# A two-layer kernel: ranking set apart from the router, two products issued in parts, and heads normalised one slot later

## The chip, the cores and the metric

The kernel runs on one core of a Trainium2 chip, as one launch. The metric is the device time in microseconds from the first to the last instruction, as a median over runs. Five engines work side by side, each through its own list of instructions: TensorE (PE, with its weight loads as PEld), VectorE (DVE), ScalarE (ACT), GpSimd (POOL) and SyncE (SP), which here only issues transfers. They wait for each other on semaphores alone.

## What is computed

Two layers over x of 8 batches, 512 rows and 128 columns, all in 32-bit floats. A layer normalises its rows, computes a sequence part s and a gate part g, and gives x + s * silu(g). In the first layer s is a state-space scan with 16 states and g a mixture of 8 experts, 2 for each row. In the second layer s is a causal attention of one head; g is a block of its own, cut to what matters here:

```
x = x + attention(rmsnorm(x, w_ln1))          # 16 heads, keys shared, causal softmax, product with Wo
residual = x
xn = rmsnorm(x, w_ln2)
probs = softmax(xn @ Wgate + expert_bias)     # 8 experts
topk_p, topk_i = top_k(probs, 2)
topk_p = topk_p / sum(topk_p)
comb = sum(one_hot(topk_i) * topk_p)
routed = einsum(comb, experts(xn))            # silu(xn @ Wg) * (xn @ Wu), then @ Wd
g = residual + shared_expert(xn) + routed
out = x_of_the_layer + s * silu(g)
```

The ratio of two softmax values does not depend on the softmax's denominator, and the order of the values doesn't either.

## The kernel before

`two_layers` has three stages with barriers between them: `route` and `experts0` (the first layer's routing and experts, and the scan of the first three batches), and `layer1`, in which the scan of batches 3 to 7 and the whole second layer run together. The change is in `layer1` and in `top_two`, which it calls.

`layer1` is written out as a list of slots, 24 for each batch (`SLOTS`), and each engine walks through the same slots in the same order, from `SLOT0` to `SLOT1`. A slot from 0 to 191 does one sixth of a quad of heads: four heads of one batch are a quad, and a batch has four quads. In each slot PE computes two score tiles into bank 1 (`scores`), two tiles from which the maxima of a quad 8 slots ahead are taken into bank 0 (`maxima`), and adds the masks to both. Then ScalarE does the exponential (L1519), and DVE the reduce of the maxima (L1709). There is one bank for each, so `scores` of the next slot waits for the exponential and `maxima` for the reduce. Every second slot PE multiplies the probabilities with the values (`weigh`, L1264).

Everything else of a batch is attached to a slot by the table `WHEN`, relative to the batch's slot 0: `due(slot, what)` gives the batch for which `what` is due in this slot. With 24 slots to a batch, an entry of 34 falls into the next batch's slot 10. In this text "loop batch n" is the slots 24n to 24n+23, and "place p" is a slot whose number modulo 24 is p. In a slot, each engine issues what is due in the order of its own code, behind the slot's scores and maxima. An engine works its list strictly in order, so that a wait holds up all that stands behind it.

What the change touches, with its place before:

- Head quads. ScalarE copies a finished quad to `o` (`take_quad`), SP copies its denominators to `dens` (`denominators`, 7 slots after the quad's first, `DENS`), DVE inverts them (L1766, 8 slots, `INVERT`), SP writes them to memory and reads them back, spread over 128 partitions (`spread_reciprocals`, 8 slots, `SPREAD`), and DVE multiplies (L1769, 10 slots, `TAKE`: places 4, 10, 16 and 22). `o` holds `HEADS_KEPT` quads.
- `attention` (29, place 5): PE waits for all four normalised quads of a batch and multiplies them with `wvo` in 32 matmuls (L1381) into bank 5; DVE adds the rows (L1809) and gives `x2`.
- `squares`, `roots2`, `scale2`, `turn2` (30, 30, 31, 32): second norm and its transpose (L1298).
- `router` (34, place 10): logits by 8 matmuls (L1408); on DVE `top_two`: bias, maximum, subtraction (L1838 to L957), ScalarE's exponential (L1590), sum, reciprocal, product (L959 to L961), the pairwise comparison and rank (L964 to L969), the gates and their normalisation (L973 to L976).
- `gates_a` to `ups_c` (38 to 41): expert products through banks 5, 6 and 7, with silus on ScalarE (L1547), which needs another table than the exponential.
- `down` (46, place 22): 40 matmuls (L1324) into bank 5, then DVE's addition to `x2` (L1882).
- `final`, `result` (47, 48) and `average1` (0): the last steps of a batch on ScalarE and DVE; DVE's result is L1885 to L1887, that of the average L1893. `store` and `fetch_x` on SP wait for the result.
- The scan on DVE: four steps in every four slots (L291, L298, L308, L315), as long as batches 3 to 7 last, up to slot 148. `SCAN_PIECES` says at which slot and through which bank its projections go; `scan_due` looks it up.

`claim(n, taker, count)` makes PE wait until the last user of bank n has read it. `late` shifts the end of batch 6 by three slots, past the last scores.

## Time and profile before

| | |
|---|---|
| median of 3 runs | 1313.63 us |
| lowest and highest run | 1307.95 and 1328.43 us |
| span of the profiled execution | 1322.4 us |
| PE busy | 1105.6 us (84%) |
| DVE busy | 976.9 us (74%) |
| ACT busy | 623.9 us (47%) |
| POOL busy | 297.1 us (22%) |

The profile is of one execution, somewhat longer than the median one. Busy time is an instruction's own time on its engine; "idle before" an instruction, and the releaser named with it, say for whom the engine stood still. Matmul ends are modelled, so small overlaps mean nothing. The second layer's slots begin at about 406 us.

### The profile page before, as it was taken

What the parts mean: (1) busy time and instruction counts of PE and PEld (TensorE: products, weight loads), DVE (VectorE), ACT (ScalarE), POOL (GpSimd) and SP (SyncE); (2) the same over time, 40 slices, a digit from 0 to 9 for tenths busy, and PEclk for the clock granted to TensorE, in tenths of its full rate; (3) what the DMA queues carried; (4) which work ended last, traced back from release to release, by engine and by line L of the source; (5) the groups of instructions that cost most, each with busy time, mean ns of one, the idle gap of its engine ahead of it and who ended that gap; (6) DMA issues with size and microseconds to landing.
All of it is one profiled execution on the core that took longest, in us unless ns stands there. A gap on an engine that the chain in (4) does not pass through costs nothing.

```text
span 1322.4 us, 19242 instructions
## 1 busy us (share of the span) xinstructions
PE 1105.6 (84%) x6765; PEld 689.4 (52%) x6765; DVE 976.9 (74%) x1514; ACT 623.9 (47%) x1111; POOL 297.1 (22%) x370
## 2 busy tenths in 40 slices
PE   7679999998767977888789888988988888898886
PEld 6567787787334434435444543543455354455353
DVE  6748878886488776986897698799889867654433
ACT  2647667663325424455346454553544543443421
POOL 2075555550313103202020320141032201000000
PEclk9779999999888878988899898998999989899898
DMA  7568777773363433253235325424533421310010
GB/s 201 162 217 250 234 221 232 231 223 100 98 127 98 113 81 95 78 118 102 64 96 120 108 77 102 119 78 111 114 112 87 102 48 34 57 42 19 17 50 8
DMA packets 91117, 150.24 MB, mean 114 GB/s; under 512 B 21032, under 2 KB 50032, under 8 KB 90960
## 3 DMA queue, kind: packets, MB, share of 16 engines
q1 hardware_dynamic: 67888, 72.33, 21.6%
q0 software_dynamic: 22976, 76.43, 19.3%
q8 instruction: 56, 0.92, 0.3%
q10 hardware_dynamic: 160, 0.26, 0.2%
q14 instruction: 37, 0.30, 0.1%
HBM read 124.33 MB, written 11.54 MB: 103 GB/s over the span
## 4 chain that ended last, share of the span: by engine, by line
PE 26%; DVE 22%; issue 9%; DMA 7%; ACT 7%; POOL 2%; another core or an unknown queue 2%; SPq 0%; DVEq 0%; POOLq 0%; ACTq 0%
PE bank L1235 5%; DVE neg_max L1709 4%; DMA rec_wide<-head_recips 3%; DVE sc_state L298 2%; ACT probs L1519 2%; PE bank L1264 2%; PE bank L1319 2%; PE bank L1381 2%; PE bank L1315 2%; PE bank L1283 2%; PE bank L1324 2%; PE bank L1241 2%; PE bank L1306 1%; ACT L1519 1%
## 5 line engine op out<-in xcount | busy, mean ns | idle before, releaser
L1519 ACT ACTIVATE probs<-bank 128x1024 f32<-128x1024 f32 (+1 forms) x192 | 169.1, 881 | 337.9 <-PE bank L1241 238.4
L1709 DVE TENSOR_REDUCE neg_max<-bank 128x2 f32<-128x1024 f32 (+3 forms) x256 | 204.2, 819 | 110.7 <-PE bank L1241 80.7
L1235 PE MATMUL bank<-q_all,kk 49*128 49x512 f32 (+3 forms) x1024 | 204.1, 498 | 49.2 <-ACT probs L1519 39.4
L212 POOL DMA_DIRECT2D sc_bc_wide<-scan_bc x128 | 73.1, 572 | 492.6 <-DVE sc_ub L291 254.7
L1235 PEld LDWEIGHTS bank<-q_all,kk 49*128 49x128 f32 x1024 | 88.1, 197 | 156.7 <-issue 66.5
L1283 PE MATMUL bank<-kr,q_all 48*128 48x512 f32 (+3 forms) x512 | 114.0, 481 | 51.3 <-DVE neg_max L1709 49.7
L779 PE MATMUL bank<-xcol,wst 128*128 128x256 f32 x624 | 149.7, 384 | 0.6 <-issue 0.6
L298 DVE TENSOR_TENSOR_SCAN sc_state<-sc_a,sc_ub 128x1024 f32<-128x1024 f32 x64 | 146.0, 2282 | 0.0
L900 POOL DMA_INDIRECT xrow<-sorted_in,token_of x78 | 103.1, 1322 | 120.5 <-PE bank L766 63.3
L779 PEld LDWEIGHTS bank<-xcol,wst 128*128 128x128 f32 x624 | 114.1, 193 | 13.6 <-issue 0.9
L1264 PE MATMUL bank<-probs,vaug 128*32 128x512 f32 (+3 forms) x1024 | 99.8, 487 | 0.0
L1283 PEld LDWEIGHTS bank<-kr,q_all 48*128 48x128 f32 x512 | 49.5, 203 | 90.4 <-DVE neg_max L1709 69.7
L925 DVE SCALAR_TENSOR_TENSOR hid<-bank,wst,gel 128x256 f32<-128x256 f32 x156 | 67.4, 474 | 37.4 <-issue 24.1
L291 DVE TENSOR_TENSOR sc_ub<-sc_u,sc_bc_wide 128x1024 f32<-128x1024 f32 x64 | 78.0, 1218 | 15.6 <-DMA sc_bc_wide<-scan_bc 13.7
L250 ACT ACTIVATE sc_a<-sc_dt,neg_a 128x511 f32<-128x511 f32 x128 | 84.2, 711 | 5.7 <-PEq L682 4.3
L795 PE MATMUL bank<-w,hid 128*128 x624 | 84.7, 279 | 0.5 <-DVE hid L925 0.5
L1663 POOL DMA_INDIRECT expert_out<-sorted_out,slot x64 | 72.0, 1125 | 55.2 <-POOLq L138 35.2
L795 PEld LDWEIGHTS bank<-w,hid 128*128 128x128 f32 x624 | 77.3, 191 | 11.4 <-issue 7.6
L854 ACT ACTIVATE gel<-bank,wst 128x256 f32<-128x256 f32 x156 | 64.5, 476 | 23.1 <-PE bank L779 21.1
L315 DVE TENSOR_TENSOR sc_y<-sc_y,sc_ub 128x1024 f32<-128x1024 f32 x56 | 68.1, 1216 | 0.0
L308 DVE TENSOR_TENSOR sc_ub<-sc_state,sc_bc_wide 128x1024 f32<-128x1024 f32 x56 | 68.0, 1215 | 0.0
L1678 POOL TENSOR_SCALAR mean_sq<-ssq 128x4 f32<-128x4 f32 x8 | 7.2, 899 | 175.6 <-ACT work_b L1576 175.2
(300 smaller groups left out, 1809.6 us busy)
## 6 DMA issues: line engine op xcount, KB each, us to landing
sc_bc_wide<-scan_bc POOLq DMA_DIRECT2D x128, 512.0 KB
wst<-in_wexp SPq DMA_DIRECT2D x39, 512.0 KB
q_all<-q_kind SPq DMA_DIRECT2D x94, 128.0 KB, 4.4
rec_wide<-head_recips SPq DMA_DIRECT2D x31, 256.0 KB
p_t<-gates_turned SPq DMA_DIRECT2D x14, 512.0 KB
sorted_out<-xrow SPq DMA_DIRECT2D x7, 640.0 KB
rows_all<-in_x SPq DMA_DIRECT2D x8, 256.0 KB, 4.4
sorted_in<-rows_all SPq DMA_DIRECT2D x8, 256.0 KB, 5.6
```

What stands on the lines that cost most here:

```text
L212: eng.dma_start(self.v["bc_wide"][:, n % 2, what, :, :], self.bc_d[b, first:first + PER, :].partition_broadcast(P)).then_inc(self.rows_in[ ...
L250: last = self.nc.scalar.activation(self.v["a"][:, n % 2, j, 1:L], self.v["dt"][:, 1:L], ACT.Exp, scale=self.neg_a[:, state:state + 1])
L291: self.nc.vector.tensor_tensor(v["ub"][:], v["u"][:].unsqueeze(1).to_broadcast([P, PER, L]), v["bc_wide"][:, n % 2, 0, :, :], ALU.mult).th ...
L298: self.nc.vector.tensor_tensor_scan(merged(v["state"][:]), merged(v["a"][:, n % 2, :, :]), merged(v["ub"][:]), 0.0, ALU.mult, ALU.add).the ...
L779: last = mm(bk(inner(m)[half])[:, i * ROWS:(i + 1) * ROWS], wst[:, w % WB, half * FF + f * P:half * FF + (f + 1) * P], xcol[:, w % 3, :], ...
L795: last = mm(bk(5)[:, r * P:(r + 1) * P], hid[:, m % 4, i, r * P:(r + 1) * P], w2[:, bass.ds(e * FF + f * P, P)], start=False, stop=(f == F ...
L900: nc.gpsimd.indirect_dma_start(out=xrow[:, m, :], out_offset=None, in_=xs[0:B * L], in_offset=bass.IndirectOffsetOnAxis(ap=t["token_of"][: ...
L1235: mm(bank[1][:, par, at:at + n], kk[rows, b % 2, kt * P:(kt + 1) * P], q_all[rows, quad // 2 % 3, pair, kt * P:L].bitcast(F32), start=(at ...
L1264: last = mm(bk(4)[row:row + 32, kt * P:L], vaug[:, b % 2, kt, :], probs[:, (6 * quad + 2 * kg + pr) % RING, par, at:at + L - kt * P], star ...
L1283: mm(bank[0][:, par, at:at + n], q_all[rows, quad // 2 % 3, pair, i * P:(i + 1) * P], kr[rows, b % 2, 0:n], start=(at == 0), stop=False)
L1519: af(probs[:, slot % RING, :, 0:width], bank[1][:, :, 0:width], ACT.Exp, scale=0.125).then_inc(s["p_ready"], 1)
L1709: last = v.tensor_reduce(neg_max[:, quad % 2, pr:4:2, i], bank[0][:, :, at:at + (i + 1) * P], AX, ALU.max, negate=True)
```

## The change

Seven edits to the order of the second layer, in one diff:

- `top_two` is divided. The shift of the logits stays with the router, which moves from 34 to 36. The rest is due at 38 (`rank`). Sum, reciprocal and product of the softmax are left out; the final normalisation of the two gates stays.
- `attention` becomes `heads_a` (27: three quads, 24 matmuls) and `heads_b` (30: the fourth quad, 8 matmuls), both into bank 5, of which only the first matmul has the start flag. The second norm's steps move one slot later.
- `INVERT`, `SPREAD` and `TAKE` become 9, 9 and 11; `HEADS_KEPT` 5, `ROWS_KEPT` 3.
- `dens` and `recs` are 128x16 in place of 32x64, and so is their copy in memory.
- `down` becomes `down_a` (46, 20 matmuls) and `down_b` (47, 20 matmuls); `final` and `result` move to 48 and 49.
- `average1` moves from 0 to 1.
- Banks: the turned rows go through 7 in place of 5, the up products through 5, 6, 7 in place of 7, 5, 6, and two scan projections leave bank 5. `turned_rows` shrinks, and the last batch's turned gates use a part of `kk`.

```diff
-        rec_d = nc.dram_tensor("head_recips", (B * 4, 32, 64), F32, kind="Internal").ap()
+        rec_d = nc.dram_tensor("head_recips", (B * 4, P, 16), F32, kind="Internal").ap()
...
-def top_two(v, dve, link, t, s, normalise, turn=0):
+def shift_logits(v, link, t, s):
+
+    prob, small = t["prob"], t["small"]
+    link(v.tensor_reduce(small[:, :, 0:1], prob[:], AX, ALU.max))
+    v.tensor_tensor(prob[:], prob[:], small[:, :, 0:1].to_broadcast([P, J, E]), ALU.subtract).then_inc(s["shifted"], 1)
+
+
+def top_two(v, dve, link, t, s, turn):
...
-    link(v.tensor_reduce(small[:, :, 0:1], prob[:], AX, ALU.max))
-    v.tensor_tensor(prob[:], prob[:], over(0), ALU.subtract).then_inc(s["shifted"], 1)
     dve.wait_ge(s["exp_ready"], turn + 1)
-    link(v.tensor_reduce(small[:, :, 1:2], prob[:], AX, ALU.add))
-    link(v.reciprocal(small[:, :, 2:3], small[:, :, 1:2]))
-    link(v.tensor_tensor(prob[:], prob[:], over(2), ALU.mult))
...
-    qk1=-6, scores1=-5, turn1=-3, average1=0,
-    attention=29, squares=30, roots2=30, scale2=31, turn2=32, router=34, gates_a=38, gates_b=39, ups_a=39, ups_b=40, ups_c=41,
-    turn_gates=41, gate_hidden=44, down=46, final=47, result=48)
+    qk1=-6, scores1=-5, turn1=-3, average1=1,
+    heads_a=27, heads_b=30, squares=31, roots2=31, scale2=32, turn2=33, router=36, rank=38, gates_a=38, gates_b=39, ups_a=39, ups_b=40, ups_c=41,
+    turn_gates=41, gate_hidden=44, down_a=46, down_b=47, final=48, result=49)
...
-HEADS_KEPT = 4
-ROWS_KEPT = 2
-
-DENS, INVERT, SPREAD, TAKE = 7, 8, 8, 10
+HEADS_KEPT = 5
+ROWS_KEPT = 3
+
+DENS, INVERT, SPREAD, TAKE = 7, 9, 9, 11
...
-        dens, recs, rec_wide = sb("dens", [32, 64]), sb("recs", [32, 64]), sb("rec_wide", [P, L])
+        dens, recs, rec_wide = sb("dens", [P, 16]), sb("recs", [P, 16]), sb("rec_wide", [P, L])
...
+                def heads_part(to, b, g, j):
+                    return mm(to[:, j * P:(j + 1) * P], o[:, (4 * b + g) % HEADS_KEPT, j * P:(j + 1) * P], wvo[:, g, :],
+                              start=(g == 0 and j == 0), stop=(g == 3 and j == J - 1))
+
...
-                    if (b := due(slot, "attention")) is not None:
+                    if (b := due(slot, "heads_a")) is not None:
                         to = claim(5, s["x2_ready"], b + 1)
+                        pe.wait_ge(s["yn_ready"], 4 * b + 3)
+                        for j in range(J):
+                            for g in range(3):
+                                heads_part(to, b, g, j)
+                    if (b := due(slot, "heads_b")) is not None:
                         pe.wait_ge(s["yn_ready"], 4 * (b + 1))
                         for j in range(J):
-                            for g in range(4):
-                                last = mm(to[:, j * P:(j + 1) * P], o[:, (4 * b + g) % HEADS_KEPT, j * P:(j + 1) * P], wvo[:, g, :], start=(g == 0), stop=(g == 3))
+                            last = heads_part(bk(5), b, 3, j)
                         last.then_inc(s["att_psum"], 1)
...
-                        up_part(b, 1, 7)
-                        up_part(b, 2, 5)
-                        up_part(b, 3, 6)
+                        up_part(b, 1, 5)
+                        up_part(b, 2, 6)
+                        up_part(b, 3, 7)
...
-                        for j in range(J):
-                            last = down_part(b, j, to)
+                        for j in range(J // 2):
+                            down_part(b, j, to)
+                    if (b := due(slot, "down_b")) is not None and b != B - 2:
+                        for j in range(J // 2, J):
+                            last = down_part(b, j, bk(5))
                         last.then_inc(s["moe_psum"], 1)
...
+                    if (b := due(slot, "rank")) is not None:
+                        if b >= 1:
+                            dve.wait_ge(s["gates_psum"], b)
+                        dve.wait_ge(s["rope_ready"], 4 * min(b + 3, B))
+                        top_two(v, dve, link, dict(prob=prob, small=small, rank=rank, gates=gates, cmp_a=cmp_a, cmp_b=cmp_b, c=c), s, b)
```

## Rows read from the trace of the kernel before

**Rows 1.** The page's part 4, the chain that ended last, shares by engine.

```profile
PE 26%; DVE 22%; issue 9%; DMA 7%; ACT 7%; POOL 2%; another core or an unknown queue 2%; SPq 0%; DVEq 0%; POOLq 0%; ACTq 0%
```

**Rows 2.** Busy time by stretches: stretch, length, then each engine, granted clock, DMA.

```profile
core 0: us, PE busy (x) PEld busy (x) DVE busy (x) ACT busy (x) POOL busy (x), PEclk, DMA share, GB/s
800.00:900.00 100.00, 86.91 (x561) 47.25 (x561) 83.51 (x124) 53.15 (x88) 22.00 (x26) 0.95 0.41 104
...
1100.00:1200.00 100.00, 88.60 (x609) 49.46 (x607) 60.96 (x106) 43.33 (x74) 4.14 (x8) 0.97 0.20 41
```

**Rows 3.** One line over the run: durations (min/median/max), first and last start.

```profile
L1519 ACT ACTIVATE probs<-bank x192: 577/1023/1036, 406.0 to 1273.1; 128x1024 f32<-128x1024 f32 x128, 128x512 f32<-128x512 f32 x64
```

**Rows 4.** Timeline, slots 82 to 84 (start, length, operation, [idle before <-releaser]).

```profile
795.78 1.13 PE L1408 MATMUL bank<-c_router,work_b 128*128 128x128 f32 x8 [0.45 <-ACT turned_rows L1531]
...
800.81 0.18 DVE L1838 TENSOR_TENSOR prob<-bank,c_bias 128x32 f32<-128x32 f32 x1
...
801.47 0.23 ACT L1590 ACTIVATE prob<-prob 128x32 f32<-128x32 f32 x1 [5.84 <-DVE prob L957]
...
802.40 0.42 DVE L964 TENSOR_TENSOR turned<-prob 128x256 f32<-128x256 f32 x1
...
805.23 0.19 DVE L976 TENSOR_TENSOR gates<-gates,small 128x32 f32<-128x32 f32 x1
805.34 1.28 DVE L1709 TENSOR_REDUCE neg_max<-bank 128x2 f32<-128x768 f32 x2
...
806.68 0.58 PE L1283 MATMUL bank<-kr,q_all 48*128 48x256 f32 x2 [2.30 <-DVE neg_max L1709]
```

**Rows 5.** Timeline of DVE and ScalarE, slots 86 and 87 (places 14 and 15).

```profile
822.57 0.54 DVE L1766 RECIPROCAL recs<-dens 32x64 f32<-32x64 f32 x1 [1.50 <-DMA dens<-o]
824.04 0.69 DVE L1709 TENSOR_REDUCE neg_max<-bank 128x2 f32<-128x512 f32 x1 [0.93 <-PE bank L1241]
...
823.03 1.28 ACT L1519 ACT_TABLE_LOAD   x1
```

**Rows 6.** Timeline of PE in loop batch 7, slots 179 and 180.

```profile
1228.76 1.13 PE L1235 MATMUL bank<-q_all,kk 49*128 49x512 f32 x4 [0.81 <-ACT probs L1519]
...
1233.11 0.58 PE L1283 MATMUL bank<-kr,q_all 48*128 48x256 f32 x2 [3.21 <-DVE neg_max L1709]
```

**Rows 7.** Timeline of PE, slot 88 (place 16).

```profile
829.85 2.84 PE L1319 MATMUL bank<-work_b,c_wu 128*128 128x512 f32 x6 [0.82 <-ACT turned_rows L1531]
```

**Rows 8.** Timeline of PE and DVE, slots 94 to 98 (places 22 to 2).

```profile
853.88 1.23 DVE L1709 TENSOR_REDUCE neg_max<-bank 128x2 f32<-128x1024 f32 x1 [0.38 <-PE bank L1241]
...
855.23 4.70 PE L1324 MATMUL bank<-c_wd,hm 128*128 128x128 f32 x40
...
859.97 0.69 DVE L1882 TENSOR_TENSOR x<-x,bank 128x512 f32<-128x512 f32 x1 [2.90 <-issue]
...
861.91 1.29 DVE L1709 TENSOR_REDUCE neg_max<-bank 128x2 f32<-128x768 f32 x2 [1.26 <-PE bank L1243]
...
873.24 0.96 DVE L1709 TENSOR_REDUCE neg_max<-bank 128x2 f32<-128x768 f32 x1 [0.72 <-PE bank L1243]
```

**Rows 9.** Timeline at place 5, in loop batch 3 and in loop batch 7.

```profile
770.88 3.81 PE L1381 MATMUL bank<-wvo,o 128*128 128x128 f32 x32 [1.29 <-DVE o L1769]
...
1205.02 0.69 DVE L1769 TENSOR_TENSOR o<-o,rec_wide 128x512 f32<-128x512 f32 x1 [2.15 <-DMA rec_wide<-head_recips]
...
1205.85 5.42 PE L1381 MATMUL bank<-wvo,o 128*128 128x128 f32 x32 [1.73 <-DVE o L1769]
```

**Rows 10.** Groups by line and shape on DVE: count, busy us, mean ns, idle before.

```profile
L1766 DVE RECIPROCAL recs<-dens 32x64 f32<-32x64 f32 x31 | 16.6, 535 | 19.1 <-DMA dens<-o 19.1
...
L1758 DVE RECIPROCAL prob<-bank 128x16 f32<-128x16 f32 x1 | 0.3, 258 | 0.7 <-PE bank L1335 0.7
```

**Rows 11.** Timeline of PE, slot 80 (place 8): transposes of the second norm's rows.

```profile
786.59 0.66 PE L1298 MATMUL bank<-c_ident,work_a 128*128 128x128 f32 x4
```

**Rows 12.** Transfers by line: count, size each, median us from issue to landing.

```profile
head_recips<-recs SPq DMA_DIRECT2D x31, 8.0 KB, 1.4
...
c_a_log<-in_a_log SPq DMA_DIRECT2D x1, 8.0 KB, 2.3
```

36 lines of the change are left out of this document (15 added, 21 removed).

## The prediction

> **What bounds the kernel now.** I read, in this order: the chain that ended last, the busy time by stretches, the list of one line over the whole run, the timeline of one loop batch (batch 3, slots 72 to 95), and the same places in the last loop batch. The chain [rows 1] has no owner: PE 26%, DVE 22%, and both hand over to each other. The stretches [rows 2] say why: between 800 and 900 us DVE is busy 83.5 of 100 us and PE 86.9 of 100. After 1100 us, where the scan has ended, DVE falls to 61 of 100 and PE stays at 88.6. The 192 slots of the second layer run from 406.0 to 1273.1 us [rows 3]: 867 us, 4.5 us a slot, 108 us for a loop batch of 24 slots. Only these slots and the tail behind them are touched; the first 406 us are not.
>
> A slot has one score bank and one bank for the maxima. PE can't write the maxima of slot s+1 before DVE has reduced those of slot s, and DVE reaches that reduce only behind everything that was queued on it in slot s-1. So a slot lasts as long as the longer of PE's and DVE's work in it, with a lag of about one slot allowed. What is to be looked for is where one of the two stands still because the other has a lump. I name a place by the slot's number modulo 24.
>
> **The change, part by part.**
>
> *Ranking (places 10 and 11 before; router at 12, ranking at 14 after).* Before, the block goes on DVE from 800.81 to 805.42 us: 4.61 us, of which 0.66 us (until ScalarE takes over at 801.47) is the shift of the logits, and 3.02 us (802.40 to 805.42) the ranking proper [rows 4]. Between them lie 0.93 us: the wait for ScalarE's exponential, and sum, reciprocal and product, which are dropped. The reduce of slot 83 stands behind all that, and PE, which has been through its own work of the slot, waits 2.30 us for it [rows 4]. ScalarE waits 5.84 us for the shifted logits before it may do the exponential of slot 83, so the scores of the next slot are late as well. After, 4.61 - 0.66 = 3.95 us leave these places. The shift comes back at place 12, with the router's eight matmuls, 1.13 us [rows 4], ahead of the queries that DVE turns there; DVE will wait about that long for the queries. 3.95 - 1.13 = 2.82 us; but PE had only 2.30 us of idleness there, and its latents and values become the longer side, so I take 2.3 us.
> The 3.02 us of ranking go to place 14. There ScalarE sets the slot: two table loads around three silus, until the exponential that follows 823.03 + 1.28 us. DVE stands idle 1.50 us, does a reciprocal of 0.54 us that moves to place 15, and stands idle 0.93 us more [rows 5]: 2.97 us of room for 3.02 us. Cost about 0.1 us. So 2.2 us in each of loop batches 1 to 6 (the first ranking falls in loop batch 1): 13.2 us. Bounds for one batch: 0.93 us (what is dropped, if the moved part pushes as much elsewhere) and 3.95 us.
> In loop batch 7 no scan, queries or latents share the places. There PE waits 0.81 us for ScalarE and 3.21 us for DVE [rows 6]: 4.0 us go.
>
> *Banks of the up products (place 16).* The first up product wants bank 7, which the turned maxima have just filled: PE waits 0.82 us for ScalarE's copy [rows 7]. With bank 5 it doesn't wait. The slot's exponential is PE's to release, and the normalisation that stood on DVE in this slot moves to place 17, in front of a slot whose length PE sets. I take the whole 0.82 us, in seven loop batches: 5.7 us. Lower bound 0.
>
> *Down product in halves (places 22, 23), result and average at place 1.* The 40 matmuls take 4.70 us, DVE waits 2.90 us for their end and then 1.26 us for the next maxima [rows 8]. Half of the product, 2.35 us, goes to place 23, which is short on PE. But a normalisation and the addition (0.69 us each, as the row of L1882) go there too, behind a scan step, and three operations of the result go to place 1, which was short and is then full on DVE. From the reduce at 853.88 to that at 873.24 us the four slots take 19.4 us. I take about half of the 2.35 us, 1.2 us, in loop batches 1 to 6: 7.2 us. Bounds 0 and 4.16 us a batch.
>
> *Heads in 3/4 and 1/4, normalised a slot later.* Before, PE waits 1.29 us for the normalised heads and does 32 matmuls in 3.81 us [rows 9]. In this stretch, though, DVE works without a gap (the average input of the next batch stands behind the normalisation), so PE's stall is beside the chain: 0 in loop batches 1 to 6, where 24 matmuls, 3/4 of 3.81 = 2.9 us, now lie in place 3 under a scan step. In loop batch 7 DVE has nothing of that kind and PE is the chain: its wait of 1.73 us goes [rows 9]. Bounds: a loss of 0.5 us a batch (place 3 becomes PE's) and a gain of 1.29 us.
>
> *Small parts.* The reciprocal has 128x16 for 32x64: 258 ns against 535 ns, both sizes being in the trace [rows 10]. 31 times 0.277 us is 8.6 us of DVE, but only those that land at places 3 and 9 lie where DVE is the chain; 15 or 16 of them, 4.3 us. Against it, the turn of the second norm's rows (0.66 us [rows 11]) now stands ahead of the queries of place 9, seven times: 4.6 us at most. I put the two together at 0. The bank swaps of the turned rows and of two scan pieces only keep clear of bank 5, now held from place 3 to 6, and a third row buffer and a fifth head buffer keep the later use from blocking the norm: 0. In the tail, where one batch runs alone, the three dropped operations are on the chain: 0.7 us.
>
> *The queues.* SyncE's order changes at places 1, 3, 9, 15 and 21: the fetch of the next rows and, behind it, the copy of the denominators now wait for the result at place 1. The reciprocal wants them two slots later, some 10 us, so I cost it at nothing; if that cover were gone, DVE's reduce of place 3 would be late next.
> The denominators' copies become 128 pieces of 64 bytes for 32 of 256. The write of the reciprocals lands in 1.4 us now, and a load of the new form, 128x16, took 2.3 us [rows 12]. I take 0.9 us more, hidden: two slots lie between inversion and use. The Trainium skill (DMA: Bandwidth & Descriptors, Specifications) says that below 512 bytes a transfer is off line rate and pays a read-modify-write; the trace has both sizes below that. By the Trainium skill the new form could only be slower; by the row the sum stays as it is unless the round trip outgrows its two slots.
>
> **The sum.** 13.2 + 4.0 + 5.7 + 7.2 + 1.7 + 0 + 0.7 = 32.5 us, from the profiled execution's span of 1322.4 us: 1289.9 us. That execution lies 0.7% above the median of the runs, 1313.6 us, whose lowest is 1308.0. So I expect 1313.6 - 32.5 = 1281 us. About 2% (26 us, below 1287.4 us) is what a measurement of this kernel can tell from no change.
>
> **The rivals.**
> 1. *DVE keeps the bound and only removed work counts.* For: DVE is busy over 83% and its lumps move, they don't vanish. Against: its waits at places 14, 22 and 23 are real idleness next to lumps. Worth 7 x 0.93 + 5.7 + 4.3 = 16.5 us: 1297 us.
> 2. *The holes close fully.* PE's stalls and DVE's both vanish, with 3.95 us a batch for the ranking, 2.35 us for the down product and the 2.4 us of loop batch 7's heads and the tail: 7 x 3.95 + 5.7 + 6 x 2.35 + 2.4 = 50 us, 1264 us. Against: PE is as busy as DVE, and can't give more than it waits.
> 3. *Slower: the denominators' round trip.* If each of the 31 trips (copy, inversion, write, broadcast) becomes 4 us longer while its slack is 2 us, DVE, in whose order the normalisation stands, waits 2 us each time: 62 - 32 = 30 us more, 1344 us. It makes the kernel slower from 1.1 us of uncovered wait a trip on. For: DVE waits for this broadcast already, 2.15 us in loop batch 7 [rows 9]. Against: 8 KB took 2.3 us in the new form, 0.9 us more and not 4 [rows 12]. The Trainium skill's rule named above speaks for it too.
> 4. *Nothing moves:* what leaves places 10 and 22 is given back at 3, 12 and 1, in slots that PE then sets. PE at 87% busy speaks for it. About 1310 us.
>
> **How the numbers follow.** Forecast 0.50 (its own range 1270 to 1291), rival 1 0.29, rival 2 0.08, rival 3 0.05, rival 4 0.08. The likeliest gives 1281 us. With 2 in 10 left out (rival 3, rival 4 and the far end of rival 2) the range is 1262 to 1305 us: below it everything would have to close, above it less than 9 us would be left. Faster by over 2% (under 1287.4): most of the forecast's 0.50, rival 2 and a little of rival 1, 0.54. Within 2%: 0.40. Slower by over 2%: rival 3 beyond its point and unforeseen waits, 0.06.
>
> **What the profile will show.** Right: no wait of PE at the reduce of place 11, ScalarE's exponential of the logits without its 5.84 us; the ranking ending within 0.2 us of the reduce of place 15; no wait for the turned maxima at place 16; DVE's wait at place 22 about halved; the heads in two groups, the second without a wait; reciprocals at 258 ns; DVE busy 86 to 88% between 800 and 900 us. Wrong: waits on the denominators or the broadcast over 20 us each in sum; place 12 longer by more than the 1.8 us of router and shift; place 3 with DVE idle over 1 us; place 1 with PE waiting for the average's bank; or a lower granted clock than the 0.95 and 0.97 of [rows 2].

## The result, and the profile after it

The changed kernel takes 1303.4 us (median of 20 runs, 1295.4 to 1310.4) against 1316.2 us before (20 runs in the same sessions). The ratio is 0.990, 95% interval 0.988 to 0.993: 12.6 us less, where the forecast was 32.5. The profiled execution has a span of 1302.6 us against 1322.4.

First the totals of the page of the changed kernel: span, busy time, and the chain that ended last, by engine.

```profile
span 1302.6 us, 19217 instructions
PE 1100.2 (84%) x6765; PEld 690.9 (53%) x6765; DVE 962.8 (74%) x1490; ACT 623.5 (48%) x1111; POOL 303.6 (23%) x370
PE 32%; DVE 15%; DMA 10%; issue 7%; ACT 6%; POOL 3%; SPq 1%; DVEq 0%; POOLq 0%; ACTq 0%
```

Against [rows 1] VectorE fell from 22% to 15% of the chain, as wanted, but TensorE rose from 26% to 32% and DMA from 7% to 10%. Which transfer it is stands in the waits of the changed kernel (us in total, times, longest), and in the page's group of its score matmuls (busy us, mean ns, idle just before, and what ended it):

```profile
PE bank L1234 <- DMA q_all<-turned_rows: 47.4, 21, 6.3
```

```profile
L1234 PE MATMUL bank<-q_all,kk 49*128 49x512 f32 (+3 forms) x1024 | 205.3, 500 | 70.8 <-DMA q_all<-turned_rows 47.4
```

TensorE waits 47.4 us in 21 places, 6.3 us at most, for the copy of the turned maxima's rows into the queries' buffer (two transfers of 4 KB, each with the rows of two heads). In the kernel before that wait was 6.0 us in three places:

```profile
PE bank L1235 <- DMA q_all<-turned_rows: 6.0, 3, 2.5
```

The rows are turned at places 4, 10, 16 and 22 and needed by the scores two slots later. The change moves neither this copy nor its user; what stood around them moved. 25.2 of the 47.4 us lie ahead of place 6, in loop batches 1 to 7; the rest lies ahead of places 0 (5.8 us), 12 (6.5 us) and 18 (9.9 us).

The longest case is ahead of place 6 of loop batch 3. SyncE's queue and TensorE, changed kernel:

```profile
758.93 0.34 SPq L1144 DMA_DIRECT2D head_recips<-recs  x1
762.17 0.57 SPq L1149 DMA_DIRECT2D rec_wide<-head_recips  x1
762.79 1.36 SPq L1133 DMA_DIRECT2D q_all<-turned_rows  x2
```

```profile
760.60 0.38 PE L1242 MATMUL bank<-mask,ident 128*128 128x256 bf16 x2
767.29 2.08 PE L1234 MATMUL bank<-q_all,kk 49*128 49x512 f32 x4 [6.31 <-DMA q_all<-turned_rows]
768.38 1.21 PE L1282 MATMUL bank<-kr,q_all 48*128 48x256 f32 x2
771.02 1.16 PE L1328 MATMUL bank<-wvo,o 128*128 128x128 f32 x8
```

ScalarE has turned the rows by 759.92, but SyncE stands in `spread_reciprocals`: it wrote the reciprocals at 758.93 and may issue their broadcast only when they have landed, at 762.17 (3.2 us, the longest of the 31; the median is 1.4 us). The rows come behind that. In the kernel before the broadcast was issued a slot earlier, and at place 5 TensorE had the 3.81 us of the heads' product [rows 9] while the rows travelled. Now 3/4 of that product lie in place 3 and 1/4 in place 6 (771.02), and place 5 is empty.

This stall has a second price. Busy time by stretches, changed kernel, columns as in [rows 2] (the granted clock is the third number from the end):

```profile
759.00:761.00 2.00, 1.98 (x25) 1.04 (x17) 2.00 (x2) 1.33 (x2) 0.00 (x0) 1.00 0.07 12
761.00:767.30 6.30, 0.01 (x2) 0.01 (x2) 6.04 (x16) 3.94 (x6) 2.48 (x4) 0.75 0.12 43
767.30:770.00 2.70, 2.70 (x10) 1.19 (x10) 1.33 (x5) 0.05 (x1) 2.20 (x4) 0.50 0.01 3
770.00:772.00 2.00, 2.00 (x18) 1.18 (x17) 1.82 (x2) 1.57 (x2) 0.00 (x0) 0.77 0.73 233
```

Before the stall TensorE has 2.4 GHz. While it stands idle the grant falls, and behind the stall it works at 0.50, which is 1.2 GHz, on the scores and maxima of place 6: four score matmuls take 2.08 us there and 1.13 us in the next slot. VectorE then waits 1.53 us for the maxima. Where [rows 2] had a clock of 0.95 and 0.97, the same stretches now have 0.93 and 0.94:

```profile
800.00:900.00 100.00, 88.67 (x568) 49.02 (x568) 81.89 (x123) 54.09 (x89) 22.90 (x27) 0.93 0.37 100
1100.00:1200.00 100.00, 92.74 (x627) 52.62 (x625) 54.55 (x88) 43.25 (x74) 1.20 (x2) 0.94 0.20 42
```

Over the whole execution the mean grant is 0.909, for 0.922 before. That isn't the doing of this wait alone: e4_invert8 below has a third of it and 0.906.

What the change was for, by contrast, is there (TensorE, ScalarE and VectorE, loop batch 3; changed kernel):

```profile
802.08 0.23 ACT L1600 ACTIVATE prob<-prob 128x32 f32<-128x32 f32 x1 [1.01 <-DVE prob L951]
814.72 0.20 DVE L975 TENSOR_TENSOR gates<-gates,small 128x32 f32<-128x32 f32 x1
816.08 0.69 DVE L1719 TENSOR_REDUCE neg_max<-bank 128x2 f32<-128x512 f32 x1 [1.16 <-PE bank L1240]
820.92 2.74 PE L1318 MATMUL bank<-work_b,c_wu 128*128 128x512 f32 x6
849.23 2.47 PE L1323 MATMUL bank<-c_wd,hm 128*128 128x128 f32 x20
852.84 2.40 PE L1323 MATMUL bank<-c_wd,hm 128*128 128x128 f32 x20
```

ScalarE waits 1.01 us for the shifted logits, not 5.84 [rows 4]; the up product has no wait, for 0.82 [rows 7]; the down product comes in halves, for 4.70 us in one piece [rows 8].

### The profile page after: what moved, and what is told of

The parts are those of the page before. It is cut to its first block, busy times and chain, and to the rows that moved or that the text cites. A ratio compares the mean times of both kernels' runs of the same rounds, so it can differ in the third digit from the quotient of the medians.

```text
span 1302.6 us, 19217 instructions
## 1 busy us (share of the span) xinstructions
PE 1100.2 (84%) x6765; PEld 690.9 (53%) x6765; DVE 962.8 (74%) x1490; ACT 623.5 (48%) x1111; POOL 303.6 (23%) x370
## 3 DMA queue, kind: packets, MB, share of 16 engines
q1 hardware_dynamic: 73840, 72.33, 22.5%
## 4 chain that ended last, share of the span: by engine, by line
PE 32%; DVE 15%; DMA 10%; issue 7%; ACT 6%; POOL 3%; SPq 1%; DVEq 0%; POOLq 0%; ACTq 0%
PE bank L1234 7%; DMA q_all<-turned_rows 5%; PE bank L1263 4%; DVE neg_max L1719 2%; PE bank L1314 2%; PE bank L1328 2%; DMA q_all<-q_kind 2%; PE bank L1282 2%; PE bank L1240 2%; ACT probs L1529 2%; DVE sc_state L298 2%; PE bank L1323 2%; POOL expert_out L1673 2%; PE bank L1242 1%; PE bank L1318 1%
## 5 line engine op out<-in xcount | busy, mean ns | idle before, releaser
L1234 PE MATMUL bank<-q_all,kk 49*128 49x512 f32 (+3 forms) x1024 | 205.3, 500 | 70.8 <-DMA q_all<-turned_rows 47.4
L1282 PE MATMUL bank<-kr,q_all 48*128 48x512 f32 (+3 forms) x512 | 119.1, 501 | 42.0 <-DVE neg_max L1719 40.7
L925 DVE SCALAR_TENSOR_TENSOR hid<-bank,wst,gel 128x256 f32<-128x256 f32 x156 | 67.5, 475 | 36.9 <-issue 23.6
L1673 POOL DMA_INDIRECT expert_out<-sorted_out,slot x64 | 77.6, 1212 | 55.1 <-POOLq L138 35.1
L854 ACT ACTIVATE gel<-bank,wst 128x256 f32<-128x256 f32 x156 | 64.5, 476 | 23.5 <-PE bank L779 21.5
```

The costliest lines, as they stand in the source:

```text
L1234: mm(bank[1][:, par, at:at + n], kk[rows, b % 2, kt * P:(kt + 1) * P], q_all[rows, quad // 2 % 3, pair, kt * P:L].bitcast(F32), start=(at ...
L1282: mm(bank[0][:, par, at:at + n], q_all[rows, quad // 2 % 3, pair, i * P:(i + 1) * P], kr[rows, b % 2, 0:n], start=(at == 0), stop=False)
L1673: g_.indirect_dma_start(out=expert_out[:, k, j, :], out_offset=None, in_=ys, in_offset=bass.IndirectOffsetOnAxis(ap=t["slot2"][:, k, b * J ...
```

## The experiments

Each ran in five rounds against the kernel before, several in one session. Ratios are to the kernel before; us are that ratio's difference from 1 times 1313.6. The median of the kernel before lay between 1304 and 1318 us in the five sessions. So a difference between two ratios from different sessions carries both intervals, 5 to 10 us in all, and takes for granted that a ratio is the same in each.

### Which part of the change loses

**One edit of the changed kernel each.** `e1_rows_first` moves the issue of the reciprocals' broadcast behind the maxima's rows:

```diff
-                        spread_reciprocals(quad)
+                        write_reciprocals(quad)
...
                         maximum_rows(quad)
+                    if (quad := quad_due(slot, SPREAD + 1)) is not None and quad < QUADS - 1:
+                        read_reciprocals(quad)
```

> The changed kernel with one change of SyncE's order: the write of the reciprocals stays in its slot, but their read back is issued one slot later, behind the copy of the maxima's rows. Theory A (the rows of the maxima, which TensorE wants two slots after they are turned, are late because the 256 KB broadcast of the reciprocals was moved to stand directly ahead of them, on the queue and on the DMA engines): TensorE's wait for q_all<-turned_rows falls from 47 to under 25 us, ratio to the kernel before 0.975 to 0.983. Theory B (the wait is the plain latency of that transfer, laid open because the slots between turn and use were emptied; the broadcast does not matter): wait within 5 us of 47, ratio 0.988 to 0.993, and the normalisation of the heads waits a little more for its broadcast, which comes 1 to 2 us later.

Measured 1.026 (1.020 to 1.032), slower than before. Both theories missed the time. TensorE's wait for the rows fell from 47.4 to 13.4 us, as by theory A, but VectorE now waited 83.4 us in 24 places for the broadcast: one slot is too short for it.

`e2_lead9` computes and turns the maxima a slot earlier; the call of `maximum_rows` also moves up in SyncE's slot, ahead of the denominators.

```diff
-LEAD = 8
+LEAD = 9
```

> The changed kernel with the maxima taken 9 slots ahead in place of 8, and their rows issued first in SyncE's slot, so that the transfer has three slots in place of two. Theory A and B alike (the transfer of the maxima's rows is where the gain went): the wait for q_all<-turned_rows goes from 47 us to under 5 us and the ratio to the kernel before is 0.965 to 0.980, up to 25 us of the 47 coming out. Theory C (the wait only stands where VectorE or TensorE would have waited anyway): the wait goes and the ratio stays at 0.986 to 0.993.

Measured 0.9986 (0.995 to 1.002): worse than the change, and outside all three theories. The wait for the rows is no longer among the longest, but the turned rows now take bank 7 in slots where others want it: TensorE waits 14.7 us for ScalarE at the transposes of L1297 and 9.6 us at L1314, and VectorE waits 22.9 us for the broadcast. These two show that the wait can be moved and still cost the same elsewhere; they don't tell the causes apart.

`e3_heads_a_5` puts the 24 matmuls in place 5 again:

```diff
-    heads_a=27, heads_b=30,
+    heads_a=29, heads_b=30,
```

> The changed kernel with the three quads' 24 matmuls at place 5, where the whole product stood before, in place of place 3; the last quad stays at place 6. Theory A/B (place 5 was the cover of the rows' transfer): TensorE's wait before the scores of place 6 shrinks by the 2.9 us of matmuls, place 3 becomes 1 us shorter; ratio 0.982 to 0.988. Theory C (heads in place 5 are work on the chain): no change or worse, 0.989 to 0.996.

`e4_invert8` inverts, writes and broadcasts a slot earlier:

```diff
-DENS, INVERT, SPREAD, TAKE = 7, 9, 9, 11
+DENS, INVERT, SPREAD, TAKE = 7, 8, 8, 11
```

> The changed kernel with inversion and spread of the reciprocals at 8 slots as before the change, only the normalisation left at 11. Theory A: the broadcast is out of the way of the maxima's rows again, the wait for them falls to under 30 us, but VectorE now waits for the denominators at places 2, 8, 14 and 20 (up to 19 us in sum, as before the change); ratio 0.978 to 0.988. Theory B: no less waiting for the rows, ratio 0.990 to 0.998.

Measured 0.9736 (0.968 to 0.979) and 0.9726 (0.967 to 0.978): each of the two edits gives 22 to 23 us, more than any of the theories had it. The wait for the rows is 33.2 us in the first and 15.9 us in the second. At place 6 both leave little of the 25.2 us (8.8 and 8.2 us). At the other three places, where no product was moved, the heads' edit leaves all (24.3 us for 22.2) and the earlier inversion 7.6 us. `g1_both` has both edits.

> The changed kernel with both single edits of the earlier runs: the first three quarters of the heads' product at place 5 for 3, and inversion and broadcast of the denominators one slot earlier (8, 8 for 9, 9). Theory A, one wait: both edits pay by the same thing, TensorE's wait for the copy of the maxima's rows (47.4 us in the changed kernel, 33.2 and 15.9 us with one edit each). Then they do not add up: the wait falls below 12 us and the ratio to before is 0.964 to 0.972, at most 8 us better than either edit alone. Theory B, two causes: the heads' edit pays because 24 matmuls leave place 3 and the slots around it are levelled, the other by the queue alone. Then they add up: 0.953 to 0.961. Theory C, the earlier inversion makes VectorE wait for denominators (25.3 us) where the heads now stand: 0.973 to 0.980.

Measured 0.9689 (0.964 to 0.974), 41 us better than before, by theory A: 5 to 6 us better than either alone, with overlapping intervals, and not the 45 us on top of the change that the two would give as a sum. Only 7.8 us of the wait are left. Its chain by engine, from the page, and its busy time from 1100 to 1200 us, at a clock of 1.00:

```profile
PE 34%; DVE 21%; issue 6%; DMA 5%; ACT 5%; POOL 2%; SPq 1%; DVEq 0%; POOLq 0%; ACTq 0%
```

```profile
1100.00:1200.00 100.00, 92.00 (x668) 51.61 (x666) 54.82 (x93) 52.31 (x82) 1.20 (x2) 1.00 0.17 36
```

**The old form of the denominators in the changed kernel**, `g2_dens32` (the buffer `rec_d` in memory likewise):

```diff
-        dens, recs, rec_wide = sb("dens", [P, 16]), sb("recs", [P, 16]), sb("rec_wide", [P, L])
+        dens, recs, rec_wide = sb("dens", [32, 64]), sb("recs", [32, 64]), sb("rec_wide", [P, L])
```

> The changed kernel with the denominators as 32x64 again; every place as in the change. Theory A: the 64-byte pieces cost nothing that is seen, and the reciprocal becomes 0.28 us longer 31 times, half of it on VectorE's path: ratio to before 0.990 to 0.996. Theory B, the small pieces hold up the queue in front of the maxima's rows: TensorE's wait for them falls from 47.4 to under 40 us and the ratio is 0.980 to 0.988.

Measured 1.0048 (1.002 to 1.008), 19 us worse than the change and outside both theories. The reciprocal takes 529 ns for 243 ns, and the write and the broadcast behind it leave that much later. The wait for the rows rises to 57.6 us. That wait, and from the transfers of `head_recips` the time to landing, both of g2_dens32:

```profile
PE bank L1234 <- DMA q_all<-turned_rows: 57.6, 22, 6.5
```

```profile
DMA to landing us min/median/max: 1.3/1.3/3.1
```

So 0.29 us more ahead of the queue is seen in the wait for the rows, 10.2 us of it; where the other 9 us of the 19 lie wasn't looked into. And the 64-byte pieces cost nothing that is seen: the write lands in 1.3 us in this form, in 1.4 us in the form of the change, and in 1.4 us in the kernel before, which has the pieces of this form [rows 12].

### What each part gives alone, on the kernel before

`f2_ranking`, the ranking alone, with its block split and its three operations dropped as in the change:

```diff
-router=34, gates_a=38
+router=36, rank=38, gates_a=38
```

> The kernel before with only the ranking moved (router at place 12, ranking at 14, sum, reciprocal and product dropped). The forecast's term is 13.2 + 4.0 us and something in the tail: ratio 0.986 to 0.988. By the changed kernel's trace the stretch from the reduce of place 10 to that of 14 was only 1.1 us shorter in a batch of 1 to 6 and 4.0 us in batch 7: 10.6 us, 0.990 to 0.994. Theory C, the ranking delivers in full where no other part has lengthened the slots around it: 0.980 to 0.985.

Measured 0.9861 (0.981 to 0.991), 18 us: the forecast's terms of 13.2 and 4.0 us. But it isn't spread as the forecast had it. From the starts of VectorE's reduces, the stretch from place 10 to 16 became shorter by 1.2, 0.2, 1.2, 1.3 and 0.8 us in loop batches 1 to 5, 4.2 us in 6, and in 7 (to place 15) by 7.3 us. In batches 1 to 5 places 10 and 11 give 2.8 to 4.5 us, and places 12 and 13, with router, shift and queries, take 0.1 to 3.2 and places 14 and 15 0.5 to 1.9 of it back. (One execution of each kernel: between two kernels that don't differ there, the same stretch differs by up to 2.1 us.)

`k1_old_ranking`, the changed kernel with the ranking put back whole at place 10:

```diff
-router=36, rank=38, gates_a=38
+router=34, gates_a=38
```

> The changed kernel with the ranking put back whole behind the router at place 10, all else as in the change. Theory A, the ranking pays in the changed kernel what it pays alone (14 to 18 us): ratio to before 1.001 to 1.006. Theory B, its gain is partly lost in the changed kernel, where a later wait for the maxima's rows sets the slot (11 us or less, as the stretch from place 10 to 14 shows): 0.993 to 1.000. Theory C, it is worth more there: over 1.008.

Measured 1.0068 (1.003 to 1.010), just above theory A's range: 21 us worse than the change. Within the intervals the ranking is worth as much inside the change as alone, so the loss isn't there. Its wait for the rows, 48.7 us, is that of the change.

`f1_banks`, the banks of the up products of place 16 alone (and the same in `hidden`):

```diff
-                        up_part(b, 1, 7)
-                        up_part(b, 2, 5)
-                        up_part(b, 3, 6)
+                        up_part(b, 1, 5)
+                        up_part(b, 2, 6)
+                        up_part(b, 3, 7)
```

> The kernel before with only the banks of the up products at place 16 changed (5, 6, 7 for 7, 5, 6). Theory A, the forecast's term: TensorE's wait of 0.82 us for the turned maxima goes in seven loop batches, 5.7 us: ratio 0.993 to 0.998. Theory B, the time goes into the next wait, for the copy of the maxima's rows that place 18 needs or for VectorE: 0.999 to 1.002.

Measured 0.9934 (0.990 to 0.997), 8.7 us: the forecast's 5.7 us, rather more.

`f3_down`, the down product alone:

```diff
-average1=0,
+average1=1,
...
-down=46, final=47, result=48)
+down_a=46, down_b=47, final=48, result=49)
```

> The kernel before with only the down product in halves (places 22, 23), result and average at place 1. Theory A, the forecast's term of 7.2 us, or the 1.7 us a batch that the changed kernel's stretch from place 22 to 2 shows: 0.990 to 0.996. Theory B, the result at place 1 holds up SyncE's queue (rows of the next batch, denominators) and VectorE as much as the halves give: 0.998 to 1.005.

Measured 1.0012 (0.998 to 1.005): nothing, as by theory B. The stretch from place 22 to 24 did become shorter by 1.6 us a batch (10.80 to 9.16 us in batch 3, 10.79 to 9.15 in batch 4, against f1_banks, in which this part is as before), but the slots from 0 to 5, with result and average at place 1, became longer: 23.9, 23.6 and 24.4 us in batches 3 to 5 against 21.5, 20.6 and 20.6. In the change, where most of the heads' product has left place 5, the same stretch isn't longer: 20.7, 21.6 and 20.0 us.

`f4_heads`, the heads alone, with the norm and the normalisation a slot later and the banks and buffers that this needs:

```diff
-attention=29, squares=30, roots2=30, scale2=31, turn2=32,
+heads_a=27, heads_b=30, squares=31, roots2=31, scale2=32, turn2=33,
...
-DENS, INVERT, SPREAD, TAKE = 7, 8, 8, 10
+DENS, INVERT, SPREAD, TAKE = 7, 8, 8, 11
```

> The kernel before with only the heads in 3/4 (place 3) and 1/4 (place 6), the normalisation one slot later, x2 and the norm one slot later, and the bank swaps and buffers that need it; inversion stays at place 8. Theory A, the forecast's miss is here: place 5 loses the 3.8 us product that covered the copy of the maxima's rows, so TensorE waits for that copy 10 to 25 us in sum and the gain of the normalisation's cover is eaten: 1.003 to 1.015. Theory B, the split costs nothing by itself and only the later inversion in front of the copy does: 0.992 to 1.000.

Measured 1.0034 (1.000 to 1.007), 4 us slower, theory A's lower end. The wait for the rows is 13.9 us in 8 places.

`h1_no_heads` has the diffs of f1, f2 and f3 together; heads and inversion are as before.

> The kernel before with ranking, banks and down halves as in the change, but the heads whole at place 5, normalised at once, denominators 32x64, inversion at place 8. The terms of the forecast for these parts: 17.2 + 5.7 + 7.2 + 0.7 = 30.8 us, 0.9765. Theory A, these parts add up and what the change lacks is lost by heads and inversion alone: 0.968 to 0.981; TensorE waits under 15 us for the copy of the maxima's rows. Theory B, the parts take from each other: 0.983 to 0.990. Ranking alone gave 0.986.

Measured 0.9829 (0.978 to 0.988), 22 us, between the two theories. The three parts alone add to 18.3 + 8.7 - 1.6 = 25.4 us, so they add up within the intervals; what makes this less than the forecast's 30.8 is the down product. The wait for the rows is 7.1 us.

**The two moves together.** Four kernels have all parts of the change and differ in these two moves alone. The cells have the time against the kernel before and TensorE's wait for the rows, in us:

| | inversion 9 slots behind | inversion 8 slots behind |
|---|---|---|
| 24 matmuls at place 3 | -12.6, 47.4 (the change) | -36.0, 15.9 (e4) |
| 24 matmuls at place 5 | -34.7, 33.2 (e3) | -40.9, 7.8 (g1) |

The waits for the rows, of e3, e4 and g1 (us, times, longest):

```profile
PE bank L1234 <- DMA q_all<-turned_rows: 33.2, 20, 4.0
PE bank L1234 <- DMA q_all<-turned_rows: 15.9, 9, 3.0
PE bank L1234 <- DMA q_all<-turned_rows: 7.8, 4, 2.7
```

Where the other move isn't made, the heads at place 3 cost 4.9 us (f4, on the kernel before, 4.5) and the later inversion 6.2 us. Both together cost 28.3 us, 17 us more than their sum. So the 22 and 23 us above are no price of one step: most of them is what the two do to each other, since the one delays the rows and the other takes away the work that would hide the delay.

**What closes the account, and what doesn't.** h1 and f4 add up to -22.5 + 4.5 = -18.0 us. The kernel with all their parts is e4, and it differs from them by the 128x16 form alone, but has -36.0. So the form would be worth 18 us there too, give or take some 10, though e4's wait for the rows is that of f4 (15.9 us for 13.9) and the form saves VectorE only 31 times 0.29 us, 9 us, of its own time. No run has the old form with the earlier inversion and the heads at place 3: what these 18 us are stays open. The sum from h1 to the change, -22.5 + 4.5 + 23.4 (from e4 to the change) - 18.9 (from g2 to the change) = -13.5 us, meets the change's -12.6 us only if the form is worth the same with either inversion.

### Why the rows come late

**Another issuing engine.** In `m1_rows_on_act` every place is that of the change; the copy of the maxima's rows is issued by ScalarE, right behind the activation that turns them.

```diff
                     af(neg_max_t[:, quad % 2, :], bk(7)[0:4 * J, 0:P], ACT.Copy).then_inc(s["nmt_ready"], 1)
+                    act.wait_ge(s["nmt_ready"], quad + 1)
+                    pair = 2 * (quad % 2)
+                    for par in range(2):
+                        row = 64 * par + KQ
+                        act.dma_start(q_all[row:row + 1, quad // 2 % 3, pair:pair + 2, :].bitcast(F32).rearrange("o h (i w) -> o (h i) w", i=J),
+                                      neg_max_t[2 * J * par:2 * J * (par + 1), quad % 2, :]).then_inc(max_in[quad % 2], 16)
```

> The changed kernel, every place as in the change; only the copy of the maxima's rows is issued by ScalarE, right behind its own copy of them, for SyncE. Theory A, the hold-up in SyncE's queue is the whole cause: TensorE's wait for that copy falls from 47.4 to under 10 us and the ratio to before is 0.962 to 0.974. Theory B, place 5 without its product and place 3 with it are a loss by themselves, whatever the queue does: 0.980 to 0.990.

`m0_before_act` has the same edit on the kernel before.

> The control: the kernel before with the same move of that one copy to ScalarE. TensorE waits 17 us for it there (matmuls and weight loads together). Theory A: at most that is to be had, ratio 0.988 to 0.998. Theory B, any kernel of this kind gains by it as much as the changed one, so that the change is not what made the wait: 0.965 to 0.980.

Measured 0.9946 (0.991 to 0.998) and 0.9956 (0.993 to 0.999). Theory A fell: the wait is still 43.3 us, and the kernel is 5 us behind the change, with overlapping intervals. It isn't the order of issues in SyncE's queue alone. Loop batch 1 of this kernel, SyncE's and ScalarE's queue, then TensorE:

```profile
533.10 0.55 SPq L1141 DMA_DIRECT2D rec_wide<-head_recips  x1
533.20 0.27 ACT L1531 ACTIVATE turned_rows<-bank 16x128 f32<-16x128 f32 x1 [0.72 <-PE bank L1283]
533.50 1.31 ACTq L1536 DMA_DIRECT2D q_all<-turned_rows  x2
538.63 2.08 PE L1224 MATMUL bank<-q_all,kk 49*128 49x512 f32 x4 [4.15 <-DMA q_all<-turned_rows]
```

The rows are issued at once, and still take until 538.63. The busy stretches there (last two columns: share of the DMA engines, GB/s) show what the engines carry meanwhile:

```profile
534.00:535.00 1.00, 0.47 (x6) 0.19 (x4) 0.96 (x3) 0.08 (x1) 0.00 (x0) 1.00 0.16 43
535.00:536.00 1.00, 0.00 (x0) 0.00 (x0) 0.97 (x2) 1.00 (x2) 0.00 (x0) 1.00 0.46 139
536.00:537.00 1.00, 0.00 (x0) 0.00 (x0) 0.97 (x4) 0.73 (x2) 0.00 (x0) 1.00 0.27 102
537.00:538.00 1.00, 0.00 (x0) 0.00 (x0) 0.97 (x7) 0.00 (x0) 0.18 (x1) 1.00 0.14 51
```

Ahead of the rows' two transfers of 4 KB stands the broadcast of 256 KB, issued 0.4 us before them. Whether it is the cause, the next pair of runs tests. The Trainium skill (DMA: Bandwidth & Descriptors, Issuing engines are not separate DMA queues) says that transfers issued by ScalarE, SyncE and GpSimd run on the same 16 DMA engines and interleave; by that rule ScalarE's issue saves sequencer time alone, and the trace agrees: in loop batch 1 the scores start 5.2 us behind ScalarE's copy, whichever of the two engines issues the rows.

**The broadcast's size.** `n1_small_wide` keeps every place, wait and issue of the change and cuts 30 of the 31 broadcasts from 128 rows to four. It leaves out the other rows of the factor, so its result is not that of the change:

```diff
+                    if quad == 0:
                         sp.dma_start(rec_wide[:, :], row.unsqueeze(1).to_broadcast([4, 32, L])).then_inc(s["rec_in"], 16)
+                    else:
+                        sp.dma_start(rec_wide[0:P:32, :], row).then_inc(s["rec_in"], 16)
```

> The changed kernel with 30 of the 31 broadcasts of reciprocals cut from 128 rows (256 KB) to four (8 KB); the other partitions of the factor keep what the first broadcast left, so the heads are normalised by old sums. Theory A, the rows wait for the broadcast's data: at place 6 the scores start 2.6 to 3.3 us behind ScalarE's copy in loop batches 1 and 4 (5.2 and 4.6 us in the changed kernel), TensorE's wait for the rows falls from 47.4 to under 32 us and the ratio to before is 0.970 to 0.982. Theory B, only the order of issues counts: these stay over 4.5 us, the wait over 40 us, 0.985 to 0.992.

> The control: the kernel before with the same 30 broadcasts cut to four rows, with the same left out. Theory A: the rows are not behind the broadcast here; only VectorE's wait for the factor (19.8 us) can fall: 0.988 to 0.999. Theory B, a smaller broadcast speeds any kernel of this kind by as much as the changed one: 0.975 to 0.985.

Measured 0.9793 (0.975 to 0.983) and, for the control, 0.9894 (0.986 to 0.993), both as by theory A. The wait for the rows fell from 47.4 to 24.3 us, and loop batch 1, with the broadcast's issue still 0.4 us ahead, has

```profile
531.36 1.13 PE L1237 MATMUL bank<-q_all,kk 49*128 49x512 f32 x4 [1.72 <-DMA q_all<-turned_rows]
```

for 4.18 us in the change. So the mechanism is shown at its place. Its price isn't: 0.9793 is 14.6 us better than the change, and the control gained 13.9 us too, where the wait for the rows only went from 6.0 to 3.8 us; there the small broadcast takes away VectorE's own wait for it (19.8 to 1.3 us). The broadcasts' share of the change's loss can't be read from this pair.

The place in all of these, ahead of the scores of place 6, in loop batches 1 to 6. Times are us behind the end of ScalarE's copy, the same point in each; the last row is TensorE standing idle.

| | before | change | m1 (rows on ScalarE) | n1 (small broadcast) | e4 (inversion 8) | g1 (both) |
|---|---|---|---|---|---|---|
| broadcast issued | -3.6 -3.3 -3.6 -4.2 -3.6 -3.6 | -0.4 -2.8 2.3 -0.8 2.0 -2.5 | -0.4 -0.6 2.2 -0.8 1.6 -2.5 | -0.4 -0.1 1.6 -0.8 1.9 -2.5 | -5.1 -6.3 -1.8 -2.9 -1.9 -5.0 | -1.6 -3.2 -2.6 -2.9 -3.0 -3.5 |
| rows issued | 0.0 in all | 0.2 0.0 2.9 0.0 2.6 0.0 | 0.0 in all | 0.2 0.5 2.2 0.0 2.5 0.0 | 0.0 in all | 0.0 in all |
| scores start | 7.0 6.6 6.9 5.8 8.1 5.9 | 5.2 2.7 7.4 4.6 7.4 3.0 | 5.2 5.3 5.3 5.3 2.5 2.8 | 2.7 3.0 4.8 4.0 5.0 2.6 | 2.6 2.6 4.0 4.0 3.8 2.6 | 4.4 3.7 4.5 4.2 3.8 3.6 |
| idle | 0 in all | 4.2 1.7 6.3 3.6 5.5 2.0 | 4.2 4.3 4.3 4.3 0.6 1.8 | 1.7 2.0 3.7 3.0 3.1 1.5 | 1.6 1.6 2.2 3.0 2.0 1.6 | 0 in all |

Three things add up. Undisturbed (e4, batches 1, 2 and 6) the scores can start 2.6 us behind the copy, and since TensorE has only 1.0 us of work left by then at an empty place 5, it stands 1.6 us. A broadcast issued within a us ahead of the rows adds 2 to 2.7 us (change, batches 1 and 4; m1, batches 1 and 2). SyncE's stand for the reciprocals adds another 2.6 to 2.9 us in batches 3 and 5. In m1, batches 3 and 4, the two issues of 0.63 us lie on ScalarE ahead of a logarithm between two table loads, so that the exponential ends only 5.2 us behind the copy and TensorE waits for that: what the queue gave there, ScalarE took. With 3/4 of the product back in place 5 (g1) TensorE works 2.9 us longer and nothing of it is seen.

### A faster version, and the down product once more

`m2_both_act` is g1_both with the rows issued by ScalarE. `m3_down_whole` is g1_both with the down product whole at place 22, result and average at place 0.

> Heads at place 5, inversion at 8, and the copy of the maxima's rows on ScalarE. Only 7.8 us of wait are left to take. Theory A: 0.961 to 0.968. Theory B, two more issues on ScalarE in front of an exponential cost what the wait was: 0.968 to 0.975.

> Heads at place 5, inversion at 8, and the down product whole again at place 22, result and average at place 0. With the halves this kernel had 0.969. Theory A, the down term is zero here too, as it was alone (1.001): 0.966 to 0.972. Theory B, the term of the forecast (7.2 us) exists once nothing later holds TensorE up: 0.973 to 0.980.

m2_both_act took 1258.5 us, ratio 0.9564 (0.952 to 0.961): 57 us faster than the kernel before, 45 us faster than the change, the fastest of all, and better than either theory had it. The rest of the wait for the rows hardly fell (7.5 us for 7.8); TensorE's wait for VectorE's reduces did, from 54.6 to 43.1 us:

```profile
PE bank L1272 <- DVE neg_max L1715: 43.1, 31, 3.3
PE bank L1224 <- DMA q_all<-turned_rows: 7.5, 5, 2.4
```

Why taking the rows out of SyncE's queue gives 16 us here (of two ratios from different sessions), 6 us in the kernel before and nothing in the change stays open. m3_down_whole measured 0.9741 (0.969 to 0.979). That is 6.8 us worse than g1_both, the size of the forecast's term, but the two intervals overlap: whether the halves are worth anything once nothing else holds TensorE up stays open.

## Why the prediction was wrong, step by step

Two steps failed, and they failed together: the heads' split, put at "0 in loop batches 1 to 6", and the order of SyncE's queue, "I cost it at nothing". Together they cost 28 us: with both, TensorE waits 47.4 us for the copy of the maxima's rows, and with neither (g1) 7.8 us. The prediction has no such wait.

*What bounds the kernel* held: PE's and DVE's lumps against each other in a slot. Where a lump left a slot in which the other engine was idle, time was gained (ranking, banks); where it came to a full one, it was given back.

*Ranking.* The sum of 17.2 us was right (18 us alone, 21 us inside the change), the working behind it wasn't. In loop batches 1 to 5 it gave 0.95 us a batch and not 2.2: that is rival 1's price of 0.93. The shift was priced at its 1.13 us of router, but places 12 and 13 gave back up to 3.2 us, and 14 and 15 more than the 0.1 us put down for them. Batch 7, put at the waits' 4.0 us, gave 7.3, batch 6 4.2. Two misses of opposite sign: that the sum fits is luck.

*Banks.* Right in mechanism and, with 8.7 us for 5.7, nearly in size.

*Down halves.* The 1.2 us a batch at places 22 and 23 were there: 1.6 us in f3, 0.5 to 1.0 us in the change. What failed is the price of place 1, "short and is then full on DVE": halving the 2.35 us was to cover it, but alone (f3) and with the heads whole at place 5 (h1) the slots 0 to 5 took the whole term back. In the change itself they aren't longer, and against g1_both the halves may be worth 6.8 us; what the term is there stays open.

*Heads.* "0 in loop batches 1 to 6" was reasoned from what the 24 matmuls would meet in place 3 and what TensorE's wait of 1.29 us at place 5 was worth. What the product itself covered at place 5 was not asked. It covered a copy issued one slot earlier, which needs 2.6 us and for which TensorE has 1.0 us of other work, and the bound for a loss, 0.5 us, was laid on the wrong slot. Alone it costs 4.5 us, in the change 22.

*The queues.* This is the other half. It was put at nothing with the fetch, the denominators and the result in view, and the later inversion was looked at only from its own user ("two slots lie between inversion and use"). But `DENS, INVERT, SPREAD` from 8 to 9 puts a write, a wait of 1.4 us for it, and a 256 KB broadcast directly ahead of `maximum_rows`, whose slot is 6 - 8 = 4 modulo 6, one slot behind. TensorE needs the rows two slots later. It costs 6 us where the heads' product stands at place 5, and 23 us where it doesn't. Without it the change is at 0.9726, 36 us. That this is near the forecast's 32.5 is luck: by the account above some 18 of the 36 us go with the form of the denominators, which the forecast had at 0.

*Small parts.* Put at 0, with the shorter reciprocal worth at most 4.3 us. In the changed kernel the form is worth 19 us. 10 of them are in the wait for the rows, since the reciprocal stands ahead of that queue. The account above says that it would be worth about as much with the earlier inversion, where that wait is small, so this isn't all of it, and the cause of the rest is open.

*The rivals.* Rival 3, the longer round trip, did not come: VectorE's wait for the broadcast fell from 19.8 to 9.2 us, and that for the denominators from 19.1 us to none, as the later inversion was to do. Rival 4 names what happened to the down product. Rival 1's time is the nearest, 1297 us, but not for its reason. None had a transfer that is late for TensorE.

*The signs.* Seen as forecast: the exponential of the logits, no wait at the up product, two head groups, the second without a wait, 243 ns for the reciprocal. The wait of 2.30 us for the reduce of place 11 is gone, but that for the reduce of place 10 rose from 0.34 to 2.0 us. Not seen: the ranking ending within 0.2 us of the reduce of place 15; it ends 0.5 to 2.1 us ahead, and VectorE waits for TensorE. Seen as warnings: place 12 longer by 2.5 to 3.4 us in three of loop batches 1 to 5, place 3 with VectorE idle 2.26 us in batch 2 and 1.92 us in batch 6, and the lower clock. VectorE's busy share between 800 and 900 us fell to 82% where 86 to 88% was to come. Over the run its reduces waited 144 us for TensorE, before 103 us.

## What to carry to other kernels

When work is moved out of a slot, list the transfers in flight during it and ask what TensorE does until they land; a product without a wait ahead of it may be the cover of somebody else's copy. When a transfer is moved by one slot, look at the next issue in its queue and at the bytes it puts into the DMA engines in front of that, not only at its own user. Price two such moves together: here each cost 5 or 6 us alone and the two 28 us. And a long stall of TensorE can be paid twice, as in loop batches 1 and 3: by the wait, and by matmuls at half the clock behind it.

## What the runs showed of the hardware

- The two 4 KB copies of the rows, issued right behind a broadcast of 256 KB, let the scores start 2 to 2.7 us later than alone, from whichever engine they are issued (in batch 1 of the change and of m1 5.2 us behind ScalarE's copy, in batch 1 of e4 2.6 us); cutting the broadcast to 8 KB gave nearly all of it back (2.7 us, batch 1 of n1).
- Two such issues occupy the issuing engine for 1.31 us (m1) to 1.36 us (the change); on ScalarE this delays the exponential behind it (m1, batches 3 and 4).
- After a stall of 6.3 us (the change, batch 3) TensorE's granted clock was 0.50 for the next 2.7 us, and after 4.18 us (batch 1) too: 2.08 us for four score matmuls. Behind a stall of 1.72 us (n1, batch 1) the same matmuls took 1.13 us, but TensorE then stood another 1.62 us, and the grant was 0.50 from 535 to 540 us.
- 8 KB landed in 1.4 us as 128 pieces of 64 bytes (the change) and in 1.3 or 1.4 us as 32 pieces of 256 bytes (g2, before).
